# Layer 3's rotary partners by DMA through a scratch array in DRAM instead of by a matmul with a permutation, and its queries and keys three tiles ahead instead of two

## The chip, the cores and the metric

One core of one Trainium2 chip runs the whole program in one launch. The metric is the device time of an execution in microseconds (us). Engines are named as in the profile: PE is the matmul engine (PEld its weight loads), DVE the vector engine, ACT the scalar engine, POOL the GpSimd engine, SP the engine that here only issues DMAs.

## The reference, cut to what matters

Four transformer-like layers run one after another over x of 64 sequences of 64 tokens of 256 features. The change is in the attention of the last of them, layer 3:

```
nx = _ada_rmsnorm(x, time_emb, w_norm1, t1_w1, t1_b1, t1_w2, t1_b2)
q = (nx @ wq + bq).reshape(b, s, N_HEADS, HEAD_DIM)       # 16 heads of 16
k = (nx @ wk + bk).reshape(b, s, N_HEADS, HEAD_DIM)
v = (nx @ wv + bv).reshape(b, s, N_HEADS, HEAD_DIM)
q = q * c + _rotate_half(q) * si                          # rotate_half: [-x2, x1] of the halves of 8
k = k * c + _rotate_half(k) * si
scores = jnp.einsum('bshd,bthd->bhst', q, k) / jnp.sqrt(jnp.float32(HEAD_DIM))
probs = jax.nn.softmax(scores, axis=-1)
attn = jnp.einsum('bhst,bthd->bshd', probs, v).reshape(b, s, D_MODEL)
x = x + attn @ wo + bo
```

Every feature of a query or key needs its partner, the feature 8 places away in the same head of 16.

## The kernel before

All arithmetic is fp32. The 4096 tokens are 32 tiles of 128 tokens (two sequences each), and the layer's attention is straight-line code, written out for the tiles t = 0 to 31. Each engine has its own instruction list, in the order in which its function writes it, and runs it in that order; engines wait for each other by semaphores. `after(engine, L.s["name"], n)` is such a wait: for the signal "name" to have been given n times. So the order of the code below is the order of the work.

In `pe_narrow`, one tile t of PE is: `scores(t)`; `project(t - 2)`, the output projection of two tiles ago; `qk(t + 2)`, queries and keys of two tiles ahead, transposed, features on the partitions, into the one PSUM bank psW1; `turn_probs(t, 0)`, transposes of the first half of the exponentials; `pe_transpose_x(t + 3)`; `values(t + 2)`; `turn_probs(t, 1)`; `rotate(t + 2)`; `outputs(t)`. `rotate` multiplies the biased queries and keys (128 x 512) with a 128 x 128 permutation, `partner`, so that every feature's partner stands on its partition, and it uses psW1 again.

In `act_narrow`, ACT does in tile t: exponentials of half 0; `biased(t + 2)`, four activations that bring psW1 to the buffer qb with the bias; exponentials of half 1; two copies of the turned exponentials to SBUF (signals pta and ptb); `values(t + 2)`, which copies the values out of PSUM; `modulate(t + 3)`, which writes the modulated, normalised input hT. In `dve_narrow`, DVE does the maxima and subtractions of both halves (`dve_softmax`), then `add`, `output`, `measure`, then `sines(t + 2)`, partner times sine, and `dve_norm(t + 4)`. In `pool_narrow`, POOL does cosine times qb, adds the product with the sine (signal qf), and spreads the keys over four head masks (signal mask), all for tile t + 2. Layer 0 runs through the same functions without the rotation.

The buffers hT, qb and qk have two copies each. SP has no DMA to issue between layer 3's loads and the stores of the last feed-forward.

Of the kernel before, what the change touches and what calls it, by code (L numbers as in the profile page):

```python
# [14 lines left out]
P = 128  # L15
# [112 lines left out]
def build_program(nc, A, out):  # L128
    ctx = ExitStack()
    with ctx:  # L130
# [90 lines left out]
        mod_rows = nc.dram_tensor("mod_rows", [B, 2 * D], FP32, kind="Internal").ap()  # L221
        slot_token = nc.dram_tensor("slot_token", [E8 * CAP], I32, kind="Internal").ap()
# [8 lines left out]
        class Attention:  # L231


            def __init__(self, li):
# [30 lines left out]
                if li == 3:  # L265
                    self.sin, self.cos = W.take(4, P), W.take(4, P)
                    self.qk = [W.take(4, P) for _ in range(2)]
                self.g, self.b = table(f"g{li}"), table(f"b{li}")
# [5 lines left out]
                                 3: " qk qke mask vp on xb rot rsin rcos qf"}[li], NT)  # L274
                if li == 1:
                    self.s |= signals("rows_in", NT * 32)
                self.loads = {0: 2, 1: 3, 2: 4, 3: 5}[li]
# [218 lines left out]
        def pe_narrow(pe, L):  # L496
# [5 lines left out]
            def qk(n):  # L502
                after(pe, L.s["h"], n + 1)
                after(pe, L.s["rsin" if rotary else "qke"], n)
                for q in range(4):
                    for k in range(KC):
                        ins = nc.tensor.matmul(psW1[:, q * P:(q + 1) * P], w[:, k, q * P:(q + 1) * P],  # L507
                                               L.hT[n % 2][:, k, :], start=(k == 0), stop=(k == KC - 1))
                ins.then_inc(L.s["qk"].sem, 1)

            def rotate(n):

                after(pe, L.s["qke"], n + 1)
                nc.tensor.matmul(psW1[:, :], partner[:, :], L.qb[n % 2].rearrange("p a b -> p (a b)"), start=True, stop=True
                                 ).then_inc(L.s["rot"].sem, 1)

            def values(n):
# [3 lines left out]
                for b in range(2):  # L521
                    for k in range(KC):
                        for hp in range(2):
                            ins = nc.tensor.matmul(psV[64 * hp:64 * hp + 64, b], L.hT[n % 2][:, k, b * N:(b + 1) * N],
# [217 lines left out]
        def dve_narrow(v, ch, L):  # L742
            rotary = L.li == 3
            def sines(n):

                after(v, L.s["rot"], n + 1)
                after(v, L.s["qf"], n)
                nc.vector.tensor_tensor(by_batch_part(L.sin), psW1[:, :].rearrange("p (a n) -> p a n", n=N), angles(1),
# [1290 lines left out]
```

## Time and profile before

| | before |
|---|---|
| time, median of 3 runs | 2900.86 us (2899.26 to 2901.13) |
| the profiled execution's own time | 2900.1 us |
| its span, first to last instruction | 2898.3 us |
| PE busy | 2621.5 us (90%) |
| DVE busy | 1624.3 us (56%) |
| ACT busy | 1045.3 us (36%) |
| POOL busy | 470.9 us (16%) |
| mean granted PE clock | 0.950 of full speed |

The profile is of one execution. Its span leaves 1.8 us of the execution's time outside. A busy share is a mean over stages with different limits, so for a change in one stage the trace of that stage is read: layer 3's attention, from about 2255 to 2536 us. Lines as L514 are lines of the kernel before. Where an instruction is an fp32 matmul, the trace has more than one record for it, so counts there are of records.

### The profile page before, as it was taken

Reading aid. Unit: us, or ns where it says so; the run is one execution under the profiler, and the core shown is the slowest. Engines: PE = TensorE matmul, PEld = TensorE weight load, DVE = VectorE, ACT = ScalarE, POOL = GpSimd, SP = SyncE. Lnnn points to the kernel's source line nnn. Section 1 sums busy time; section 2 is a strip of 40 time slices with the busy share of each in tenths; the row PEclk is TensorE's granted clock in tenths of the full one; section 3 lists DMA queues with packets and bytes.
Section 4 is the critical chain, followed back from the end, with each engine's and each line's share of the span. In section 5 each row is a group of like instructions: output and inputs, shape, how many; then the busy total and the mean of one; then the engine's idle time right before and its main releaser. Section 6 shows DMA issues by size and latency. Waiting matters only on the chain.

```text
span 2898.3 us, 60070 instructions
## 1 busy us (share of the span) xinstructions
PE 2621.5 (90%) x24108; PEld 1838.6 (63%) x24108; DVE 1624.3 (56%) x3749; ACT 1045.3 (36%) x2095; POOL 470.9 (16%) x402
## 2 busy tenths in 40 slices
PE   6888599999999843999799999997999899889999
PEld 5666366666666532666688888885444677646555
DVE  5888677878777576332355555543332688732221
ACT  4555355655655400212133333332121566510110
POOL 2233010101101001223111111110000566400000
PEclk9999799999999955999899999998999899989999
DMA  5000000000000121333400000000000000000000
GB/s 200 2 2 2 12 23 22 29 29 22 29 22 29 52 84 54 92 92 91 124 0 0 0 0 0 0 0 1 0 0 0 2 2 2 2 8 8 14 15 15
DMA packets 62439, 78.27 MB, mean 27 GB/s; under 512 B 12704, under 2 KB 52128, under 8 KB 61792
## 3 DMA queue, kind: packets, MB, share of 16 engines
q1 hardware_dynamic: 56160, 67.88, 7.1%
q0 software_dynamic: 6144, 8.52, 1.5%
q8 instruction: 92, 1.51, 0.2%
q14 instruction: 43, 0.35, 0.0%
HBM read 59.33 MB, written 17.06 MB: 26 GB/s over the span
## 4 chain that ended last, share of the span: by engine, by line
PE 83%; DVE 10%; ACT 3%; issue 3%; DMA 1%; SPq 0%; POOL 0%; DVEq 0%; POOLq 0%; ACTq 0%
PE psW L301 16%; PE psW L294 8%; PE psS L1268 7%; PE psP L416 4%; PE psP L1234 4%; PE psP L1228 4%; PE psS L1262 4%; PE psO L1228 4%; PE psP L409 4%; PE psO L1234 4%; PE psW L507 3%; PE psS L360 3%; PE psO L393 2%; PE psO L325 2%; PE psP L376 2%
## 5 line engine op out<-in xcount | busy, mean ns | idle before, releaser
L301 PE MATMUL psW<-r,work 128*128 128x512 f32 x1024 | 482.1, 604 | 1.0 <-DVE work L718 1.0
L1162 POOL TENSOR_TENSOR work<-work 128x512 f32<-128x512 f32 x128 | 132.2, 1044 | 1151.8 <-DVE work L740 1151.8
L301 PEld LDWEIGHTS psW<-r,work 128*128 128x128 f32 x1024 | 180.9, 191 | 162.8 <-issue 157.1
L294 PE MATMUL psW<-work,r 128*128 128x128 f32 x2048 | 244.6, 278 | 1.0 <-DVE work L718 1.0
L294 PEld LDWEIGHTS psW<-work,r 128*128 128x128 f32 x2048 | 235.9, 194 | 3.5 <-DVE work L718 1.4
L729 DVE TENSOR_REDUCE work<-psS 128x8 f32<-128x512 f32 x256 | 175.5, 686 | 107.5 <-PE psS L537 74.7
L1268 PE MATMUL psS<-r,work 128*128 128x256 f32 x960 | 211.2, 381 | 5.3 <-DVE work L1338 5.3
L1268 PEld LDWEIGHTS psS<-r,work 128*128 128x128 f32 x960 | 181.2, 190 | 32.8 <-DVE work L1338 6.1
L731 DVE TENSOR_TENSOR work<-psS,work 128x512 f32<-128x512 f32 x256 | 177.1, 692 | 11.3
L1084 ACT ACTIVATE work<-work 128x512 f32<-128x512 f32 x128 | 80.1, 626 | 277.4 <-DVE work L731 277.4
L1140 POOL TENSOR_TENSOR work<-work,head_mask 128x1024 f32<-128x1024 f32 x64 | 121.5, 1899 | 205.2 <-ACT work L1024 202.7
L1418 ACT ACTIVATE work<-psP 128x512 f32<-128x512 f32 x64 | 38.2, 597 | 285.6 <-PE psO L1228 285.6
L1338 DVE TENSOR_TENSOR work<-work,psO 128x512 f32<-128x512 f32 x64 | 44.1, 689 | 168.7 <-ACT work L1418 168.7
L416 PEld LDWEIGHTS psP<-work,r 128*128 128x128 f32 x1024 | 123.8, 195 | 16.2 <-ACT work L1100 8.8
L507 PEld LDWEIGHTS psW<-work,r 128*128 128x128 f32 x1024 | 125.3, 196 | 12.1 <-ACT work L1004 5.9
L507 PE MATMUL psW<-work,r 128*128 128x128 f32 x1024 | 128.9, 280 | 4.3 <-ACT work L1004 3.8
L1040 ACT ACTIVATE work<-work 128x512 f32<-128x512 f32 x128 | 81.1, 634 | 139.7 <-DVE work L731 139.7
L716 DVE TENSOR_TENSOR work<-psW,tab 128x256 f32<-128x256 f32 x64 | 27.0, 421 | 184.6 <-PE psW L287 184.6
L416 PE MATMUL psP<-work,r 128*128 128x128 f32 x1024 | 126.6, 278 | 1.2 <-ACT work L1100 1.2
L409 PE MATMUL psP<-r,work 128*128 128x256 f32 x512 | 126.1, 380 | 1.2 <-ACT work L1100 1.2
L1234 PE MATMUL psP<-work,r 128*128 128x512 f32 x256 | 120.7, 611 | 4.7 <-DVE work L1327 3.0
L1228 PE MATMUL psP<-work,r 128*128 128x512 f32 x256 | 122.2, 600 | 3.0 <-DVE work L1327 3.0
(222 smaller groups left out, 4681.8 us busy)
## 6 DMA issues: line engine op xcount, KB each, us to landing
r<-in_l_fc SPq DMA_DIRECT2D x16, 1024.0 KB, 6.7
work<-mod_rows SPq DMA_DIRECT2D x64, 128.0 KB, 2.8
r<-in_l_w SPq DMA_DIRECT2D x2, 3072.0 KB, 14.8
x<-in_x SPq DMA_DIRECT2D x8, 512.0 KB, 9.6
gather_table<-work SPq DMA_DIRECT2D x32, 128.0 KB, 1.8
moe_sum<-work SPq DMA_DIRECT2D x32, 128.0 KB, 1.7
x<-moe_sum SPq DMA_DIRECT2D x8, 512.0 KB, 7.3
out<-x SPq DMA_DIRECT2D x8, 512.0 KB, 2.9
```

The lines of the kernel that those rows point to most:

```text
L294: ins = nc.tensor.matmul(ps[:, q * P:(q + 1) * P], w[:, k, lo + q * P:lo + (q + 1) * P], L.hT[:, k, :], start=(k == 0), stop=(k == KC - 1))
L301: ins = nc.tensor.matmul(ps[:, 0:width], L.hT[:, k, :], w[:, k, lo:lo + width], start=(k == 0), stop=(k == KC - 1))
L409: ins = nc.tensor.matmul(psP[:, 0:D], L.oT[:, j, :], l1_wout[:, j, :], start=(j == 0), stop=(j == FJ - 1))
L416: ins = nc.tensor.matmul(psP[:, q * P:(q + 1) * P], l2_wout[:, j, q * P:(q + 1) * P], L.oT[:, j, :], start=(j == 0), stop=(j == FJ - 1))
L507: ins = nc.tensor.matmul(psW1[:, q * P:(q + 1) * P], w[:, k, q * P:(q + 1) * P], L.hT[n % 2][:, k, :], start=(k == 0), stop=(k == KC - 1))
L729: ch.link(nc.vector.tensor_reduce(mx, ps, AX.X, ALU.max))
L731: nc.vector.tensor_tensor(L.E[:, 8 * i:8 * i + 8, :], ps, mx.unsqueeze(2).broadcast_to([P, 8, N]), ALU.subtract).then_inc(L.s[f"sub{i}"].s ...
L1140: nc.gpsimd.tensor_tensor(L.kbd[n % 2], k.unsqueeze(2).broadcast_to([P, 4, 4, N]), head_mask[:, 8:12].unsqueeze(1).unsqueeze(3).broadcast_ ...
L1162: nc.gpsimd.tensor_tensor(E, E, halves(L.rs)[i].unsqueeze(2).broadcast_to([P, 8, N]), ALU.mult).then_inc(L.s[f"prob{i}"].sem, 1)
L1228: ins = nc.tensor.matmul(ps, w[:, k, j * P:(j + 1) * P], Q.gT[:, k, :], start=(k == 0), stop=(k == KC - 1))
L1234: ins = nc.tensor.matmul(HB[j % 4], Q.w1[u][:, k, j * P:(j + 1) * P], Q.gT[:, k, :], start=(k == 0), stop=(k == KC - 1))
L1268: ins = nc.tensor.matmul(psS[:, r * D:(r + 1) * D], Q.hid[:, j, r * P:(r + 1) * P], Q.w2[u][:, j, :], start=(j == 0), stop=(j == FJ - 1))
```

## The change

For tiles 2 to 31 the product with the permutation is gone. SP waits for the biased queries and keys of tile n, stores them twice into a scratch array `rotated` in DRAM, so that each head's 16 rows stand there twice in a row, waits for both stores, and loads 16 rows from 8 further down: each feature's partner comes back to its partition, in the new buffer `turned`. DVE's `sines` reads it there, from SBUF instead of from PSUM. Tiles 0 and 1 keep the product. The distance `L.far` by which queries and keys go ahead becomes 3 in layer 3 (it stays 2 in layer 0): hT and qb get three copies, `qk`, `biased` and `modulate` are each called for one tile further ahead, and so are the transposes of x and `dve_norm`. The calls for tile 2 come before the loop. `values` stays two tiles ahead, but in layer 3 it is written after `turn_probs(t, 1)`, where `rotate` was. ACT's order within a tile stays.

```diff
+        rotated = nc.dram_tensor("rotated", [2, 8, 32, 4 * P], FP32, kind="Internal").ap()
...
-                    self.hT = [W.take(KC, P) for _ in range(2)]
-                    self.qb = [W.take(4, P) for _ in range(2)]
+                    self.far = 2 if li == 0 else 3
+                    self.hT = [W.take(KC, P) for _ in range(self.far)]
+                    self.qb = [W.take(4, P) for _ in range(self.far)]
...
+                    self.turned = [W.take(4, P) for _ in range(2)]
...
             def qk(n):
                 after(pe, L.s["h"], n + 1)
-                after(pe, L.s["rsin" if rotary else "qke"], n)
+                after(pe, L.s["qke"], n)
+                if rotary and n <= 2:
+                    after(pe, L.s["rsin"], n)
...
             if rotary:
                 rotate(1)
+                qk(2)
+                pe_transpose_x(pe, L, 3)
...
             for t in range(NT):
                 scores(t)
                 if t > 1:
                     project(t - 2)
-                if t + 2 < NT:
-                    qk(t + 2)
+                if t + L.far < NT:
+                    qk(t + L.far)
                 turn_probs(t, 0)
-                if t + 3 < NT:
-                    pe_transpose_x(pe, L, t + 3)
-                if t + 2 < NT:
+                if t + L.far + 1 < NT:
+                    pe_transpose_x(pe, L, t + L.far + 1)
+                if t + 2 < NT and not rotary:
                     values(t + 2)
                 turn_probs(t, 1)
                 if t + 2 < NT and rotary:
-                    rotate(t + 2)
+                    values(t + 2)
                 outputs(t)
...
             def sines(n):
-                after(v, L.s["rot"], n + 1)
+                if n < 2:
+                    after(v, L.s["rot0"], n + 1)
+                    turned = psW1[:, :].rearrange("p (a n) -> p a n", n=N)
+                else:
+                    after(v, L.s["rot_odd" if n % 2 else "rot_even"], n // 2 * 16)
+                    turned = by_batch_part(L.turned[n % 2])
...
             def biased(n):
                 after(a, L.s["qk"], n + 1)
-                after(a, L.s["qf" if L.li == 3 else "s1"], n - 1)
+                after(a, L.s["qf" if L.li == 3 else "s1"], n + 1 - L.far)
...
             values(1)
+            if L.li == 3:
+                biased(2)
+                modulate(3)
...
                 exps(t, 0)
-                if L.li == 3 and t + 2 < NT:
-                    biased(t + 2)
+                if L.li == 3 and t + 3 < NT:
+                    biased(t + 3)
                 exps(t, 1)
...
+            for n in range(2, NT):
+                u = n % 2
+                after(sp, L[3].s["qke"], n + 1)
+                back = L[3].s["rot_odd" if u else "rot_even"]
+                after(sp, back, (n // 2 - 1) * 16)
+                for copy in range(2):
+                    sp.dma_start(rotated[u, :, 16 * copy:16 * copy + 16, :], rows_of(L[3].qb[n % 3])
+                                 ).then_inc(L[3].s["rot_rows"].sem, 16)
+                after(sp, L[3].s["rot_rows"], (n - 1) * 32)
+                after(sp, L[3].s["rsin"], n - 1)
+                sp.dma_start(rows_of(L[3].turned[u]), rotated[u, :, 8:24, :]).then_inc(back.sem, 16)
```

Where this puts the instructions is seen in the two programs' lists. Line numbers differ between them: `scores`, `project`, `qk`, `turn_probs`, `values`, `outputs` are L537, L572, L507, L547, L524, L557 and L562 before, and L546, L581, L516, L556, L533, L566 and L571 in the change; the product is L514 before, L523 in the change; the transposes of x are L287 and L294. PE, a tile in the middle of layer 3, before, from the first turn of the exponentials to `outputs`:

```order
L547 MATMUL psP<-consts,work 128x128 [waits pta,exp0]
L547 MATMUL psP<-consts,work 128x128 x3
L287 MATMUL psW<-consts,work 128x128 [waits h,xn]
L287 MATMUL psW<-consts,work 128x128
L524 MATMUL psO<-r,work 64x128 [waits xupd,v]
L524 MATMUL psO<-r,work 64x128 x7
L547 MATMUL psP<-consts,work 128x128 [waits ptb,exp1]
L547 MATMUL psP<-consts,work 128x128 x3
L514 MATMUL psW<-work,partner 128x512 [waits qke]
L557 MATMUL psO<-work,pair_sums 32x128 [waits pta,ptb,on,v]
```

The same place of PE's list in the change:

```order
L556 MATMUL psP<-consts,work 128x128 [waits pta,exp0]
L556 MATMUL psP<-consts,work 128x128 x3
L294 MATMUL psW<-consts,work 128x128 [waits h,xn]
L294 MATMUL psW<-consts,work 128x128
L556 MATMUL psP<-consts,work 128x128 [waits ptb,exp1]
L556 MATMUL psP<-consts,work 128x128 x3
L533 MATMUL psO<-r,work 64x128 [waits xupd,v]
L533 MATMUL psO<-r,work 64x128 x7
L566 MATMUL psO<-work,pair_sums 32x128 [waits pta,ptb,on,v]
```

The product is gone, and the eight matmuls of the values stand behind the second turn, the one that waits for exp1, instead of ahead of it.

ACT, the same tile in the change (L1060 exponentials, L1040 `biased`, L1071 the copies, L1032 the values' copies, L1020 `modulate`):

```order
L1060 ACTIVATE work<-work 128x512 [waits sub0]
L1040 ACTIVATE work<-psW,col 128x128 [waits qf,qk]
L1040 ACTIVATE work<-psW,col 128x128 x3
L1060 ACTIVATE work<-work 128x512 [waits sub1]
L1071 ACTIVATE work<-psP 128x512 [waits pv,ta]
L1071 ACTIVATE work<-psP 128x512 [waits pv,tb]
L1032 ACTIVATE heads_v<-psO 64x16x16 [waits pv,vp]
```

Nothing moved in this list within a tile: `biased`, which waits for the signal of `qk`, still stands between the two exponentials; it is now that of tile t + 3.

PE ahead of the first tile, in the change, from `values(1)` to the first tile's `qk`:

```order
L533 MATMUL psO<-r,work 64x128 x7
L523 MATMUL psW<-work,partner 128x512 [waits qke]
L516 MATMUL psW<-work,r 128x128 [waits rsin,qke,h]
L516 MATMUL psW<-work,r 128x128 x7
L294 MATMUL psW<-consts,work 128x128 [waits h,xn]
L294 MATMUL psW<-consts,work 128x128
L546 MATMUL psS<-work 64x256 [waits mask,su_consts,su_bias]
L546 MATMUL psS<-work 64x256 x7
L516 MATMUL psW<-work,r 128x128 [waits qke,h]
```

The first `scores` (L546) stood right behind the product before; now the `qk` of tile 2, with a wait for rsin, and the transposes of tile 3 stand between.

## Rows read from the trace of the kernel before

**Rows 1.** The chain that ended last, by line, 2366 to 2392 us.

```profile
by line: PE psW L507 20.8%; PE psS L537 14.0%; PE psO L572 12.2%; PE psW L514 9.9%; ACT work L1024 9.8%; PE psO L557 8.8%; PE psP L547 7.6%; PE psO L562 6.9%; ACT work L1040 6.1%; issue 4.2%
```

**Rows 2.** Busy time per window; columns: window, length, engines, PE clock, DMA.

```profile
2350.00:2400.00 50.00, 49.55 (x720) 38.13 (x716) 40.03 (x68) 32.89 (x89) 31.22 (x25) 1.00 0.01 2
```

**Rows 3.** Timeline of one tile, PE: start, length, engine, line, what.

```profile
2375.06 1.09 PE L537 MATMUL psS<-work 64*64 64x256 f32 x16
...
2377.05 1.95 PE L507 MATMUL psW<-work,r 128*128 128x128 f32 x16
...
2378.83 0.60 PE L547 MATMUL psP<-consts,work 128*128 128x128 f32 x4
...
2379.27 0.38 PE L287 MATMUL psW<-consts,work 128*128 128x128 f32 x2
...
2379.58 1.09 PE L524 MATMUL psO<-r,work 128*64 128x128 f32 x16
...
2380.75 0.66 PE L547 MATMUL psP<-consts,work 128*128 128x128 f32 x4
...
2381.25 1.02 PE L514 MATMUL psW<-work,partner 128*128 128x512 f32 x2
...
2382.20 0.65 PE L557 MATMUL psO<-work,pair_sums 128*32 128x128 f32 x16
...
2383.22 1.09 PE L537 MATMUL psS<-work 64*64 64x256 f32 x16
```

**Rows 4.** The same tile, ACT.

```profile
2379.03 1.15 ACT L1024 ACTIVATE work<-psW,col 128x128 f32<-128x128 f32 x4 [0.75 <-PE psW L507]
...
2380.05 0.64 ACT L1040 ACTIVATE work<-work 128x512 f32<-128x512 f32 x1
...
2381.45 0.60 ACT L1051 ACTIVATE work<-psP 128x512 f32<-128x512 f32 x1 [0.26 <-PE psP L547]
...
2381.94 0.76 ACT L1016 ACTIVATE heads_v<-psO 64x256 f32<-64x256 f32 x2
...
2382.72 1.30 ACT L1004 ACTIVATE work<-psW,tab 128x64 f32<-128x64 f32 x4
```

**Rows 5.** The same tile, DVE: `sines`, and the next tile's first maximum.

```profile
2382.36 0.69 DVE L748 TENSOR_TENSOR work<-psW,consts 128x512 f32<-128x512 f32 x1 [0.41 <-PE psW L514]
...
2384.37 0.69 DVE L729 TENSOR_REDUCE work<-psS 128x8 f32<-128x512 f32 x1 [1.05 <-PE psS L537]
```

**Rows 6.** Timeline of tile 1, PE: `values`, then the second turn.

```profile
2281.78 1.09 PE L524 MATMUL psO<-r,work 128*64 128x128 f32 x16
...
2282.81 0.66 PE L547 MATMUL psP<-consts,work 128*128 128x128 f32 x4
```

**Rows 7.** Start of the layer: `scores` of tiles 0 and 2, and `sines(1)`.

```profile
2270.12 1.09 PE L537 MATMUL psS<-work 64*64 64x256 f32 x16
...
2270.23 0.69 DVE L748 TENSOR_TENSOR work<-psW,consts 128x512 f32<-128x512 f32 x1 [1.03 <-PE psW L514]
...
2285.28 1.09 PE L537 MATMUL psS<-work 64*64 64x256 f32 x16
```

**Rows 8.** End of the layer: `scores` of tiles 30 and 31.

```profile
2513.81 1.09 PE L537 MATMUL psS<-work 64*64 64x256 f32 x16
...
2521.27 1.09 PE L537 MATMUL psS<-work 64*64 64x256 f32 x16
```

**Rows 9.** DMA issues: count, KB each, median us to landing.

```profile
out<-x SPq DMA_DIRECT2D x8, 512.0 KB, 2.9
...
consts<-in_consts SPq DMA_DIRECT2D x1, 297.5 KB, 2.7
```

**Rows 10.** Timeline of layer 0: PE behind a gap.

```profile
71.12 1.12 PE L547 MATMUL psP<-consts,work 128*128 128x128 f32 x4 [2.69 <-ACT work L1040]
```

**Rows 11.** Two windows of layer 0; the 1.00 or 0.50 is the granted clock.

```profile
71.00:74.40 3.40, 3.28 (x22) 2.72 (x22) 3.33 (x5) 1.18 (x3) 0.00 (x0) 0.50 0.00 0
76.00:100.00 24.00, 21.73 (x330) 17.76 (x329) 18.86 (x34) 15.72 (x43) 7.74 (x6) 1.00 0.01 2
```

More of the change, by code:

```diff
@@ L273, in __init__ @@
                                  2: " prob0 prob1 rsum0 rsum1 i0 i1 i2 i3 e0 e1 e2 e3 v0 v1 v0e ote yt bk",
-                                 3: " qk qke mask vp on xb rot rsin rcos qf"}[li], NT)
+                                 3: " qk qke mask vp on xb rsin rcos qf"}[li], NT)
                 if li == 1:
                     self.s |= signals("rows_in", NT * 32)
+                if li == 3:
+                    self.s |= signals("rot0", 2)
+                    self.s |= signals("rot_rows", (NT - 2) * 32)
+                    self.s |= signals("rot_even rot_odd", (NT - 2) // 2 * 16)
                 self.loads = {0: 2, 1: 3, 2: 4, 3: 5}[li]
@@ L507, in qk @@
                         ins = nc.tensor.matmul(psW1[:, q * P:(q + 1) * P], w[:, k, q * P:(q + 1) * P],
-                                               L.hT[n % 2][:, k, :], start=(k == 0), stop=(k == KC - 1))
+                                               L.hT[n % L.far][:, k, :], start=(k == 0), stop=(k == KC - 1))
                 ins.then_inc(L.s["qk"].sem, 1)
@@ L513, in rotate @@
                 after(pe, L.s["qke"], n + 1)
-                nc.tensor.matmul(psW1[:, :], partner[:, :], L.qb[n % 2].rearrange("p a b -> p (a b)"), start=True, stop=True
-                                 ).then_inc(L.s["rot"].sem, 1)
+                nc.tensor.matmul(psW1[:, :], partner[:, :], L.qb[n].rearrange("p a b -> p (a b)"), start=True, stop=True
+                                 ).then_inc(L.s["rot0"].sem, 1)
             def values(n):
@@ L523, in values @@
                         for hp in range(2):
-                            ins = nc.tensor.matmul(psV[64 * hp:64 * hp + 64, b], L.hT[n % 2][:, k, b * N:(b + 1) * N],
+                            ins = nc.tensor.matmul(psV[64 * hp:64 * hp + 64, b], L.hT[n % L.far][:, k, b * N:(b + 1) * N],
                                                    wv[:, k, :, hp, :], start=(k == 0), stop=(k == KC - 1))
@@ L1000, in modulate @@
                 after(a, L.s["a"], n + 1)
-                after(a, L.s["vp"], n - 1)
+                after(a, L.s["vp"], n + 1 - L.far)
                 for k in range(KC):
                     for b in range(2):
-                        ins = nc.scalar.activation(L.hT[n % 2][:, k, b * N:(b + 1) * N],
+                        ins = nc.scalar.activation(L.hT[n % L.far][:, k, b * N:(b + 1) * N],
                                                    psW0[:, k * P + b * N:k * P + (b + 1) * N], ACT.Identity,
@@ L1021, in biased @@
                 after(a, L.s["qk"], n + 1)
-                after(a, L.s["qf" if L.li == 3 else "s1"], n - 1)
+                after(a, L.s["qf" if L.li == 3 else "s1"], n + 1 - L.far)
                 for q in range(4):
-                    ins = nc.scalar.activation(L.qb[n % 2][:, q, :], psW1[:, q * P:(q + 1) * P], ACT.Identity,
+                    ins = nc.scalar.activation(L.qb[n % L.far][:, q, :], psW1[:, q * P:(q + 1) * P], ACT.Identity,
                                                bias=c(f"l{L.li}_bqk", q))
@@ L1056, in act_narrow @@
                     values(t + 2)
-                if t + 3 < NT:
-                    modulate(t + 3)
+                if t + L.far + 1 < NT:
+                    modulate(t + L.far + 1)
         def act_attention(a, L):
```

11 lines of the change are left out of this document (6 added, 5 removed).

## The prediction

> **What bounds the kernel now.** I looked first at the stage alone, since the change touches only layer 3's attention. In a window of it PE is busy 49.55 of 50 us at the full clock, 1.00, which is 2.4 GHz [rows 2]. Read alone, that says that PE is the limit and that every matmul taken off it is won. The chain of work says something else: the product L514 has 9.9% of it, but 9.8% and 6.1% belong to ACT's L1024 and L1040 [rows 1]. So PE is released by ACT once per tile, and I read one tile in order of time to see where.
>
> From one `scores` to the next is 8.16 us [rows 3]. The steps, each the distance between two starts [rows 3, 4]: `scores` and `project`, 2375.06 to 2377.05, 1.99; `qk` until ACT can begin `biased`, to 2379.03, 1.98; `biased` until the second exponential, to 2380.05, 1.02; that exponential and the hop to PE's second turn, to 2380.75, 0.70; the turn until the product, 0.50; the product until `outputs`, 0.95; `outputs`, 1.02. The sum is 8.16, the whole tile. `values` is not in it. It runs from 2379.58, beside ACT's part, and would let the second turn begin 1.03 later, about 2380.61 [rows 3, 6]; the exponential ends at 2380.69. PE looks full because two limits lie 0.1 us apart: the time PE would need by itself, and the path `qk`, `biased`, exponential, turn.
>
> **The change, part by part.**
>
> *A tile in the middle.* The product and its 0.95 leave PE. But ACT's order stays: `biased`, which waits for this tile's `qk`, stands ahead of the second exponential, so the second turn stays 1.98 + 1.02 + 0.70 behind the start of `qk`. That `biased` now serves a tile further ahead changes nothing in this wait. `values` moves from the place where it hid in that path to one behind the turn, and takes the product's place on it. So instead of 0.50 + 0.95 the path has a turn followed by `values`. The turn: four transposes take 0.44 to the next start when more transposes follow, and two take 0.31 when `values` follows, 0.09 more than their half of 0.44 [rows 3]; so 0.53. `values`: 1.03 to the next start [rows 6]. A tile becomes 8.16 + 0.03 + 0.08 = 8.27. No row shows `values` followed by `outputs`. From below, `outputs` can't start before ACT's last copy ends at 2382.05, which with a hop of 0.06 is 0.09 earlier than now [rows 3, 4]: 8.07. From above I allow another 0.1: 8.37. I take 8.27, since `values` and the transposes keep their rows whoever is next.
>
> *What else hangs on the moved work.* ACT's copies of the values can begin 0.95 later, near 2382.4 instead of 2381.94, and with `modulate` (0.76 + 1.30) end near 2384.4; the next `qk` needs them at 2385.3, the next `project` the copies alone at 2384.3 [rows 3, 4]. Both hold, by 0.9 and more. `sines` no longer waits 0.41 for the product [rows 5]; DVE is ready early anyway (1.05 of waiting before the next maximum), so this is worth nothing. It costs nothing that qb and hT have a third copy. POOL gets its input earlier.
>
> *The DMAs.* They cost nothing while their path is short enough. It starts when `biased` ends (2380.18) and must end when DVE comes to `sines` in the next tile (2381.95 plus a tile of 8.27) [rows 4, 5]: 10.0 us. Two stores of 256 KB each: as many bytes as one store of 512 KB, 2.9 us, and about 0.5 for the second issue. The load: 2.7 us for 297.5 KB [rows 9]. Sum 6.1. From below it can't matter; from above, were all of the 5.6 us of landing streaming and the rate halved, 11.7.
>
> The Trainium skill has a rule against this part (DMA: Bandwidth & Descriptors, "Why a DMA increments its semaphore by 16 and not by 1"): a DMA is spread over the largest number of engines up to 16 that divides the slowest dimension of both sides. The scratch side here is 8 x 16 x 512, so by it 8 engines would carry each of these DMAs. No row here shows such a DMA. By the rule the path lies between 6.1 and 11.7, and the sum stays as it is.
>
> *The start.* Before the first `scores` there is now `qk(2)`, which waits for `sines(1)`, over at 2270.92 [rows 7], and then 1.78 of `qk` and 0.31 of transposes [rows 3]. `scores(0)` moves from 2270.12 to 2273.1. In tile 0, `qk(3)` waits for `modulate(3)`, which on ACT stands behind `biased(2)`: 2271.0 + 1.98 + 1.15 + 1.30 = 2275.4 [rows 4]. From there the path is 1.98 + 1.02 + 0.70 + 0.53 + 1.03 + 1.02 = 6.28: `scores(1)` at 2281.7. In tile 1, `qk(4)` waits for `modulate(4)`, behind the copies of values that moved: values are done at 2280.7, plus 0.76 and 1.30 is 2282.8; 6.28 more gives `scores(2)` at 2289.1. Before, it was 2285.28 [rows 7]. Loss 3.9. Bounds: 2.2 if only the added `qk` and transposes counted, 5 if the waits cost more hops.
>
> *The end.* The last `qk` is now in tile 28. Tile 29 then looks like tile 30 before, which took 7.46 instead of 8.16 [rows 8]. Gain 0.7; nothing, if `values(31)` isn't hidden in it.
>
> *Sum.* Tiles 2 to 28 are 27: 27 x 0.11 = +3.0. With the start, +3.9, and the end, -0.7: +6.2 us. The profiled execution took 2900.1 by its own time: 2906.3. The median of the runs is 0.8 higher: **2907**. A measurement of this kernel tells about 0.2%, 5.8 us, from no change; the forecast lies just beyond that, a slight loss.
>
> **The rivals.**
>
> *Faster: PE was the limit.* If the second turn follows the transposes as soon as PE is free, a tile loses the product: 8.16 - 0.95 = 7.21. Then 27 x -0.95, +3.9 and -0.7 give -22: 2878. For it: [rows 2]. Against: the turn starts 0.06 after the exponential ends, and ACT is in the chain in every tile. It decides if ACT could do `biased` without waiting for the same tile's `qk`. 6 in 100.
>
> *The tile gets no longer.* If `outputs` follows the last copy, 8.07: -2.4 + 3.9 - 0.7, a result of 2902. Part of the forecast's own range, 2901 to 2911.
>
> *The DMAs come late.* The loop that closes: path, `sines` and the norm (2.01 less 1.05 of waiting, 0.96), then from the maximum to the end of `biased` (2384.37 to 2388.34, less 0.75 of waiting, 3.2): 4.2 in all, within two tiles, 16.5 [rows 4, 5]. So a path over 12.3 us makes every tile longer by half of what is over: at 14 us, 0.85 x 29 = +25, with the rest 2931. The upper bound above is 11.7. 7 in 100.
>
> *The clock falls.* With `values` gone from there, PE stands still from 2379.58 to 2380.75 in every tile, 1.17 us, where it waited 0.1 before [rows 3]. In layer 0 it idled 2.69 us and then ran at clock 0.50, 1.2 GHz, for 3.4 us [rows 10, 11]; with 2.3 us of idling in 24 the clock was 1.00. The new gaps are between, and nearer to the second. A fall costs up to 1.7 us: in five tiles +8.5, 2916; in all 27, 2953. 8 in 100. The Trainium skill (TensorE: Matmul & The Clock Gate, "A second HAM failure mode: psum-queue depth-cycling") tells of a kernel in which short idles between groups of matmuls, often enough, made the clock go up and down; layer 0's window at 1.00 shows that such idling doesn't do it always.
>
> **How the numbers follow.** Forecast 0.79, of its range about 0.43 above 2906.7 and 0.36 below; late DMAs 0.07 and clock 0.08 slower; PE the limit 0.06 faster. Slower 0.58, same 0.36, faster 0.06. The range 2900 to 2916 takes in the forecast's bounds and a clock that falls in a few tiles.
>
> **What would show it.** In the trace after: tiles 8.27 apart; a gap of about 1.1 us on PE before the second turn, released by ACT's exponential; `values` between it and `outputs`; `biased` still released by `qk`; `sines` waiting for nothing; `scores(2)` 4 us later; clock 1.00. Wrong would be: a second turn that doesn't wait for ACT, DVE idle before `sines`, or a clock under 1.00.

## The result, and the profile after

The changed kernel takes 2910.79 us (median of 7 runs, 2906.41 to 2913.19); the kernel before, beside it, 2899.26 (7 runs, 2897.55 to 2901.55). The ratio is 1.0038, interval 1.0027 to 1.0048: slower, and by more than the 0.2% that a measurement can tell. The forecast was 2907, 6.2 above before; the loss is 11.5. The profiled execution took 2912.28, 12.2 more than that of before.

The page of the kernel after: busy time of each engine (first row), the group of the two turns of the exponentials (second: busy, mean ns | idle before, and what ended it), and the new DMAs (count, KB each).

```profile
PE 2600.9 (89%) x24048; PEld 1833.6 (63%) x24048; DVE 1622.3 (56%) x3749; ACT 1048.7 (36%) x2095; POOL 469.5 (16%) x402
...
L556 PE MATMUL psP<-consts,work 128*128 128x128 f32 x512 | 84.2, 289 | 58.3 <-ACT work L1060 58.3
...
rotated<-work SPq DMA_DIRECT2D x60, 256.0 KB
...
work<-rotated SPq DMA_DIRECT2D x30, 256.0 KB
```

The second row counts both layers that run through this line: 58.3 us in which PE stands still, with the turn next in its list, until ACT's exponential is over. 37.9 of them lie between 2250 and 2540, in layer 3; the kernel before waits 4.2 us there for the same thing.

PE in a tile in the middle, after (start, length, engine, line, what, in brackets the idle time ahead and what ended it); the answer of before is [rows 3].

```profile
2375.73 1.09 PE L546 MATMUL psS<-work 64*64 64x256 f32 x16
2376.76 1.13 PE L581 MATMUL psO<-r,work 128*128 128x256 f32 x4
2377.72 1.95 PE L516 MATMUL psW<-work,r 128*128 128x128 f32 x16
2379.51 0.60 PE L556 MATMUL psP<-consts,work 128*128 128x128 f32 x4
2379.95 0.38 PE L294 MATMUL psW<-consts,work 128*128 128x128 f32 x2
2381.42 0.66 PE L556 MATMUL psP<-consts,work 128*128 128x128 f32 x4 [1.10 <-ACT work L1060]
2382.01 1.09 PE L533 MATMUL psO<-r,work 128*64 128x128 f32 x16
2383.03 0.64 PE L566 MATMUL psO<-work,pair_sums 128*32 128x128 f32 x16
2383.49 0.63 PE L571 MATMUL psO<-work,heads_v 128*32 128x64 f32 x32
2384.05 1.09 PE L546 MATMUL psS<-work 64*64 64x256 f32 x16
```

ACT in the same tile, after ([rows 4] before):

```profile
2379.71 1.14 ACT L1040 ACTIVATE work<-psW,col 128x128 f32<-128x128 f32 x4 [0.75 <-PE psW L516]
2380.73 0.64 ACT L1060 ACTIVATE work<-work 128x512 f32<-128x512 f32 x1
```

From `scores` to `scores` it is 8.32, by the starts 1.99 + 1.99 + 1.02 + 0.69 + 0.59 + 1.02 + 1.02: the path through `qk`, `biased`, exponential and second turn that the prediction draws, with the 1.10 of standing still just where `values` used to be.

SP's DMAs and DVE's `sines` with the next maximum, after ([rows 5] before):

```profile
2380.88 1.20 SPq L1913 DMA_DIRECT2D rotated<-work  x2
2386.36 0.60 SPq L1917 DMA_DIRECT2D work<-rotated  x1
```

```profile
2385.20 0.69 DVE L740 TENSOR_REDUCE work<-psS 128x8 f32<-128x512 f32 x1 [1.59 <-PE psS L546]
...
2390.98 0.69 DVE L764 TENSOR_TENSOR work<-work,consts 128x512 f32<-128x512 f32 x1
```

The stores are issued at 2380.88, the load only 5.5 later, and `sines`, which needs the load, begins 10.1 after the stores without a wait.

The start of the layer, after: PE, then DVE ([rows 7] before). The first `scores` is 18.2 behind the layer's first transposes; before it was 15.1.

```profile
2274.43 1.09 PE L546 MATMUL psS<-work 64*64 64x256 f32 x16
2276.70 2.05 PE L516 MATMUL psW<-work,r 128*128 128x128 f32 x16 [1.17 <-ACT work L1020]
...
2283.13 1.09 PE L546 MATMUL psS<-work 64*64 64x256 f32 x16
...
2288.33 0.66 PE L556 MATMUL psP<-consts,work 128*128 128x128 f32 x4 [1.91 <-ACT work L1060]
...
2292.51 1.09 PE L546 MATMUL psS<-work 64*64 64x256 f32 x16
```

```profile
2285.33 0.69 DVE L764 TENSOR_TENSOR work<-work,consts 128x512 f32<-128x512 f32 x1 [7.02 <-DMA work<-rotated]
...
2286.20 0.68 DVE L740 TENSOR_REDUCE work<-psS 128x8 f32<-128x512 f32 x1
```

In tile 0 DVE stands for 7.02 us in `sines(2)`, until the first load has landed. Tile 1's maximum is behind it in DVE's list and comes at 2286.20, though its `scores` began at 2283.13, and PE's turns of tile 1 wait in their turn. That is a wait which the prediction does not have.

Where the 12.2 us of the two profiled executions lie, in distances between starts of PE:

| stretch | before | after | difference |
|---|---|---|---|
| ahead of layer 3 (its first transposes) | 2255.02 | 2256.21 | +1.2 |
| to `scores(0)` | 15.10 | 18.22 | +3.1 |
| tile 0 | 7.58 | 8.70 | +1.1 |
| tile 1 | 7.58 | 9.38 | +1.8 |
| 27 tiles in the middle | 8.16 | 8.32 | +4.3 |
| tile 29 | 8.16 | 7.46 | -0.7 |
| tile 30 | 7.46 | 8.31 | +0.9 |
| behind `scores(31)` | 377.0 | 377.5 | +0.5 |

The first row is not the change: nothing ahead of layer 3 differs, and over the profiled executions of the kernels below these first transposes stand between 2249.5 and 2256.6. So the experiments are also compared by the length of the layer, from its first transposes to `scores(31)`: 266.3 before, 276.8 after. Each such length is from one profiled execution. Where the DMAs don't make the tiles uneven it repeats (276.8 and 276.7 in the kernel after and e2, 274.6 in e4 and e7); in the others it is one sample.

### The profile page after: what moved, and what is told of

Same layout as the page of the kernel before. It is cut to its first block, busy times and chain, and to the rows that moved or that the text cites. A ratio compares the mean times of both kernels' runs of the same rounds, so it can differ in the third digit from the quotient of the medians.

```text
span 2910.5 us, 60096 instructions
## 1 busy us (share of the span) xinstructions
PE 2600.9 (89%) x24048; PEld 1833.6 (63%) x24048; DVE 1622.3 (56%) x3749; ACT 1048.7 (36%) x2095; POOL 469.5 (16%) x402
## 4 chain that ended last, share of the span: by engine, by line
PE 83%; DVE 10%; issue 3%; ACT 3%; DMA 1%; SPq 0%; POOL 0%; DVEq 0%; ACTq 0%; POOLq 0%
PE psW L308 16%; PE psW L301 8%; PE psS L1288 7%; PE psP L423 4%; PE psP L1254 4%; PE psP L1248 4%; PE psS L1282 4%; PE psP L416 4%; PE psO L1248 4%; PE psO L1254 4%; PE psW L516 3%; PE psS L367 2%; PE psO L400 2%; PE psO L332 2%; PE psP L383 2%
## 5 line engine op out<-in xcount | busy, mean ns | idle before, releaser
L742 DVE TENSOR_TENSOR work<-psS,work 128x512 f32<-128x512 f32 x256 | 176.9, 691 | 11.3
L556 PE MATMUL psP<-consts,work 128*128 128x128 f32 x512 | 84.2, 289 | 58.3 <-ACT work L1060 58.3
L516 PEld LDWEIGHTS psW<-work,r 128*128 128x128 f32 x1024 | 125.3, 196 | 14.6 <-ACT work L1020 9.4
L516 PE MATMUL psW<-work,r 128*128 128x128 f32 x1024 | 129.0, 280 | 6.0 <-ACT work L1020 4.8
L1060 ACT ACTIVATE work<-work 128x512 f32<-128x512 f32 x128 | 81.1, 633 | 134.7 <-DVE work L742 134.6
L1254 PE MATMUL psP<-work,r 128*128 128x512 f32 x256 | 120.7, 611 | 4.7 <-DVE work L1347 3.0
## 6 DMA issues: line engine op xcount, KB each, us to landing
rotated<-work SPq DMA_DIRECT2D x60, 256.0 KB
work<-rotated SPq DMA_DIRECT2D x30, 256.0 KB
```

The lines of the kernel that those rows point to most:

```text
L742: nc.vector.tensor_tensor(L.E[:, 8 * i:8 * i + 8, :], ps, mx.unsqueeze(2).broadcast_to([P, 8, N]), ALU.subtract).then_inc(L.s[f"sub{i}"].s ...
L1254: ins = nc.tensor.matmul(HB[j % 4], Q.w1[u][:, k, j * P:(j + 1) * P], Q.gT[:, k, :], start=(k == 0), stop=(k == KC - 1))
```

## The experiments

Theory A, that of the prediction: the middle tile is bound by the path `qk`, `biased`, exponential, turn, because ACT's `biased` stands ahead of the second exponential; what left PE was not on it, and `values`, put behind the turn, is. B: PE by itself is the limit. C: the DMAs cost the time, by their waits or by what they load. Four kernels, run together (before 2897.23, 23 runs):

**e1_exp_first**, the kernel after, ACT's order swapped:

```
                 exps(t, 0)
+                exps(t, 1)
                 if L.li == 3 and t + 3 < NT:
                     biased(t + 3)
-                exps(t, 1)
```

> The changed kernel with ACT's second exponential ahead of the four activations that bring queries and keys out of PSUM, nothing else. Path theory (the second exponential waits behind them, and they wait for this tile's queries and keys): the exponential ends about 1.05 us earlier in a tile, the second turn no longer waits for it, and the next limit is ACT's copies, now behind those activations: a tile of about 7.8 us instead of 8.32, some 14 us less than the changed kernel. Rival, the DMA path of 9.8 us sets the tile: it now starts 0.5 us later, so a tile stays at 8.3 or gets longer, and DVE waits for the DMA in every tile. Rival, PE's own work is the limit: 8.3, no change.

Measured: 2900.14 (10 runs), 1.0009 of before (1.0000 to 1.0019); layer 269.7. Most middle tiles are 7.72, but eight are 7.85 to 11.3, and tile 1 is 12.05. The waits in the layer, and DVE's in tile 0:

```profile
DVE work L764 <- DMA work<-rotated: 33.9, 27, 6.9
```

```profile
2279.41 0.69 DVE L764 TENSOR_TENSOR work<-work,consts 128x512 f32<-128x512 f32 x1 [6.91 <-DMA work<-rotated]
```

A is confirmed by the 7.72, 0.60 less per tile from ACT's order alone. But the tile is now short enough for the DMAs to be late: 27 waits, where the kernel after has 6. The longest tiles, 12.05 and 11.3, hold a second cost. While PE stood still for 2.88 us ahead of the first turn of tile 1, the granted clock fell to 0.50 and stayed there for 6.8 us (the window below lies in them). In the tile of 11.3 it was at 0.50 for 3.4 us.

```profile
2282.00:2288.00 6.00, 5.59 (x62) 4.69 (x66) 4.03 (x6) 4.15 (x12) 4.52 (x4) 0.50 0.30 81
```

**e2_dead_product**, the kernel after with a product of the same size, whose result nobody reads, between transposes and second turn:

```
                     pe_transpose_x(pe, L, t + L.far + 1)
+                if rotary and t + 2 < NT:
+                    for i in range(2):
+                        nc.tensor.matmul(psW0[:, 256:512], partner[:, :],
+                                         L.qb[(t + 2) % 3][:, 2 * i:2 * i + 2, :].rearrange("p a b -> p (a b)"),
+                                         start=True, stop=True)
```

> The changed kernel with the permutation product put back on PE, in two halves into an unused part of a PSUM bank, right behind the transposes of x, that is in the gap ahead of the second turn; nobody reads it. Path theory: the gap is 1.10 us and the product takes 0.95, so the tile stays at 8.32, at most 8.4, 0 to 2 us in all. Rival, PE's own work is the limit: 0.95 us more in each of 30 tiles, +28 us.

Measured: 2909.97 (5 runs), 1.0042 (1.0027 to 1.0056); the middle tile is 8.32 again, the layer 276.7. The turn's wait went down to 0.23 instead, in this kernel's timeline of PE:

```profile
2375.82 0.59 PE L616 MATMUL psW<-work,partner 128*128 128x256 f32 x2
2376.65 0.66 PE L556 MATMUL psP<-consts,work 128*128 128x128 f32 x4 [0.23 <-ACT work L1065]
```

B falls for the changed kernel: the product costs nothing where PE waits.

**e3_values_back**, the kernel after with `values` ahead of the second turn:

```
-                if t + 2 < NT and not rotary:
+                if t + 2 < NT:
                     values(t + 2)
                 turn_probs(t, 1)
-                if t + 2 < NT and rotary:
-                    values(t + 2)
                 outputs(t)
```

> The changed kernel with the values' matmuls ahead of the second turn again, where they stood before. Path theory: they hide in the 1.10 us gap, and the path has the turn and ACT's last copy in place of the turn and the values: a tile of 8.07 to 8.1, 6 to 7 us less than the changed kernel, which is the tile of before or slightly under it. Rival, the DMA path sets the tile: no change, 8.32.

Measured: 2906.83 (10 runs), 1.0033 (1.0023 to 1.0042); middle 8.14, layer 272.7, 4.1 less than the changed kernel where 6 to 7 were expected. In its timeline `outputs` now waits for ACT's last copy:

```profile
2377.17 0.64 PE L566 MATMUL psO<-work,pair_sums 128*32 128x128 f32 x16 [0.78 <-ACT work L1069]
```

So with the product gone and `values` back in its place the tile goes from 8.16 to 8.14: the product had hidden behind ACT's copies too. The copy starts 2376.43 and takes 0.60; `outputs` starts 0.14 behind its end, where I had counted with 0.06.

**e4_no_dma**, the kernel after without the scratch array; `sines` reads qb itself, so tiles 2 to 31 get wrong partners (the rotation is left out):

```
-            for n in range(2, NT):
...
-                    after(v, L.s["rot_odd" if n % 2 else "rot_even"], n // 2 * 16)
-                    turned = by_batch_part(L.turned[n % 2])
+                    after(v, L.s["qke"], n + 1)
+                    turned = by_batch_part(L.qb[n % 3])
```

> The changed kernel without its 90 DMAs: the sine product of tiles 2 to 31 reads the queries and keys themselves instead of their partners, so the rotation is left out of the result for these tiles. Path theory: the tile in the middle stays at 8.32; only the wait of 7.02 us in tile 0, which makes tile 1 take 9.38, goes: about 1.7 us less in all. Rival, the DMAs lengthen every tile (by a wait, or by slowing the engines): the tile falls to 8.16 or under, 5 us less or more.

Measured: 2906.61 (7 runs), 1.0032 (1.0020 to 1.0043); middle 8.32, tile 1 7.66 instead of 9.38, layer 274.6. In the middle the DMAs cost nothing; at the start they cost 1.7. In the changed kernel C holds for tile 1 alone. The other 0.4 of the layer's 2.2 is in tile 30, 7.95 for 8.31, in which the clock fell to 0.50 in both.

The next four, together (before 2897.33, 22 runs):

**e5_before_exp_first**, the kernel before with the same swap on ACT (`exps(t, 1)` ahead of `biased(t + 2)`).

> The kernel before with ACT's second exponential ahead of the four activations that bring queries and keys out of PSUM; the product stays on PE. If PE's own work was the other limit, 0.1 us under the path through ACT, a tile becomes 8.06 instead of 8.16, about 3 us less in all. If the path through ACT was the only limit that mattered, much more: 7.5 or so per tile, 15 us less.

Measured: 2898.38 (10 runs), 1.0000 (0.9991 to 1.0010); middle 8.02, layer 263.4, 2.9 less than before. The gain of the layer, 0.1%, is below what the whole time can show. Here B is true: with ACT out of the way PE has no gap left.

```profile
2300.00:2500.00 200.00, 200.00 (x2800) 155.38 (x2800) 163.55 (x274) 132.37 (x350) 127.61 (x101) 1.00 0.01 2
```

So 8.02 is what PE needs by itself with the product, and a tile below it is to be had only by taking work off PE.

**e6_exp_first_no_dma**, e1 without DMAs as in e4 (the rotation of tiles 2 to 31 left out).

> The changed kernel with the second exponential first and without the 90 DMAs (the sine product of tiles 2 to 31 reads the queries and keys themselves, so the rotation is left out there). What remains with neither the product nor the DMA path. If the DMA path is what makes the tiles of the run with the exponential first irregular (up to 12.05 us), they are now even, 7.7 us or, where ACT's copies don't limit, down to 7.5; layer 3 gets some 10 us shorter than there. If ACT and PE make them so, nothing changes.

Measured: 2890.56 (10 runs), 0.9976 (0.9967 to 0.9986); all middle tiles but one 7.72 or 7.73 (the one 7.91), tile 1 7.72, layer 258.2. What made e1 uneven were its DMAs: 11.5 us of layer. The falls of the clock are in this number: without the DMAs the clock stays at 1.00 from 2264 to 2512.

**e7_product_tile2**, the kernel after with tile 2's partners from the product (into the second half of psP, so that tile 0's second turn waits for `sines(2)`), the DMAs from tile 3 on:

```
+                if rotary and t == 0:
+                    rotate(2)
...
-            for n in range(2, NT):
+            for n in range(3, NT):
```

> The changed kernel with tile 2 done by the product as well, in another PSUM bank, in PE's gap in tile 0, so that the DMAs begin with tile 3. Theory: DVE's wait of 7.02 us in tile 0 goes and tile 1 takes 7.7 us instead of 9.38, all else stays: 1.7 us less than the changed kernel. Rival: the start of the layer is slow for another reason, tile 1 stays over 9.

Measured: 2907.92 (7 runs), 1.0033 (1.0020 to 1.0045); tiles 0 and 1 are 8.70 and 7.66, middle 8.32, layer 274.6. The rotation is whole here, and tile 1 is as short as without DMAs: its 1.7 was the wait in tile 0.

**e8_longer_path**, the kernel after with a third store of 256 KB per tile, ahead of the load (with a larger scratch array and the signal's count to match):

```
-                for copy in range(2):
-                    sp.dma_start(rotated[u, :, 16 * copy:16 * copy + 16, :], ...
+                for v, copy in ((u, 0), (2 + u, 0), (u, 1)):
+                    sp.dma_start(rotated[v, :, 16 * copy:16 * copy + 16, :], ...
```

> The changed kernel with a third store of 256 KB per tile, into a spare array that nobody reads, between the two, which the load waits for too. The path from the queries to DVE gets about 2 us longer, near 11.9. By the loop worked out in the prediction a tile gets longer only over about 12.3: DVE waits up to 1.8 us in each tile, and a tile stays at 8.32 or up to 8.4. If the path has no room beyond the 0.3 us that the changed kernel's trace shows ahead of the sine product, a tile becomes longer by 1 to 2 us, 27 to 50 in all.

Measured: 2925.05 (one run, the profiled one); layer 293.8. Fourteen of the 27 middle tiles stay 8.32, but tile 1 is 13.2 and the other thirteen are 8.4 to 11.1. DVE's waits between 2300 and 2500:

```profile
DVE work L764 <- DMA work<-rotated: 44.9, 22, 3.5
```

Half a hit. From the stores' issue to `sines` the path is now 11.2 to 13.7. In the middle waits of up to 2.2 us, with a path of 12.3, left the tile at 8.32, which is where the prediction's loop puts the limit. But the loop gives half of what is over, 0.3 for the three paths of 12.9 to 13.0 in a row (2331.9 to 2350.4), and the tiles behind them took 1.1, 1.0 and 2.4 more. In the last of these the clock had fallen to 0.50 (2368.5 to 2371.9), as in tile 1. So the loop has the limit about right and the cost above it too low.

Then the versions that the runs pointed to. **e9_best** is e1 and e7 together (before 2900.20, 15 runs).

> The changed kernel with two edits: ACT does the second exponential ahead of `biased`, and tile 2's partners come from the product again (into psP, which is free there), so that the scratch array starts with tile 3. From the runs so far: a tile in the middle 7.72 from one `scores` to the next as in e6_exp_first_no_dma, tile 1 7.7 instead of 9.38, no wait of DVE for a DMA in tile 0, and from the first `scores` of the layer to the last some 240 us as in e6 against about 251 before. That would be 8 to 11 us under the kernel before, 0.996 to 0.997 of it. The rival: the DMAs' path of 9.8 us has, with tiles of 7.72, less room than in the changed kernel, so DVE still waits for the load in many tiles and the clock falls after the longer gaps, as in e1_exp_first; then the time stays at that of the kernel before or of e1, 0.998 to 1.001. The difference between the two is in the number of waits of DVE for the load: none or few, or again some 27.

Measured: 2895.96 (11 runs), 0.9984 (0.9975 to 0.9993); tile 1 is 7.72, but seven middle tiles are 0.13 to 3.0 over, the layer 264.9. The rival came true, in part: 28 waits for the load. Behind the longest of them, in the row below, comes the tile of 10.76, with the clock at 0.50 from 2490.9 to 2494.3.

```profile
2485.82 0.69 DVE L768 TENSOR_TENSOR work<-work,consts 128x512 f32<-128x512 f32 x1 [3.07 <-DMA work<-rotated]
```

The last three ran together (before 2900.03, 22 runs). **e10_norm_first** is e9 with DVE's `dve_norm(t + L.far + 2)` ahead of `sines(t + 2)`.

> e9_best with DVE's norm of tile t + 5 (0.35 us) ahead of `sines`, so that the load has 0.35 us more before DVE waits for it and before the next tile's maximum is late. In e9_best the middle tiles were 7.72 but for seven that were 0.13 to 3.0 over, 7.1 us in all. If the DMAs' path is what lengthens these, those over by little vanish and the others lose up to 0.35 each: about 2 us less in the layer, 262 to 264 from its first transposes to the last `scores`. If something else does, nothing changes (265).

Measured: 2896.95 (11 runs), 0.9993 (0.9984 to 1.0003). The middle tiles' excess fell from 7.1 to 3.8 us and the waits from 30.8 to 21.8, but tile 0 rose to 8.83 and the clock fell in the end tiles (tile 29 9.60): layer 265.0, nothing won. Why tile 0 rose is in the trace: the norm, now ahead, waits 1.24 us for PE's transposes, `sines(2)` ends 6.1 behind `scores(0)` instead of 4.5, and PE's second turn waits 1.14 for it.

**e11_four_ahead** is e9 with queries and keys four tiles ahead:

```
-                    self.far = 2 if li == 0 else 3
+                    self.far = 2 if li == 0 else 4
...
                 pe_transpose_x(pe, L, 3)
+                qk(3)
+                pe_transpose_x(pe, L, 4)
...
                 biased(2)
                 modulate(3)
+                biased(3)
+                modulate(4)
```

> e9_best with queries and keys four tiles ahead instead of three (four copies of hT and qb, one more `qk` and turn ahead of the first `scores`), so that the DMAs have a whole tile more. If their path of 9.8 us is what makes e9_best's tiles uneven, DVE waits for no load and all middle tiles are 7.72, as in e6_exp_first_no_dma where there were no DMAs. The start costs another 2.9 (the first `scores` at 21.0 behind the layer's first transposes instead of 18.1), one tile more at the end is 7.46. The layer then: 258.2 + 2.9 - 0.3 = 261 from the first transposes to the last `scores`, against 264.9 in e9_best and 266.3 before; the time 3 to 4 us under e9_best's. If the uneven tiles are not from the DMAs, they stay, and the layer is 267.

Measured: 2897.41 (11 runs), 0.9993 (0.9984 to 1.0002). All 26 full tiles are 7.71 or 7.72, and DVE never waits for a DMA: the DMAs' path was the cause of the uneven ones. But the layer is 264.8, since the start took 24.2 and not 21.0. Its timeline of PE, and a window in it (its 0.50 is the granted clock):

```profile
2275.50 3.38 PE L516 MATMUL psW<-work,r 128*128 128x128 f32 x16 [2.19 <-ACT work L1027]
...
2279.24 1.14 PE L546 MATMUL psS<-work 64*64 64x256 f32 x16
```

```profile
2276.10:2279.30 3.20, 3.20 (x20) 2.87 (x18) 0.00 (x0) 0.38 (x2) 0.14 (x1) 0.50 0.00 0
```

The added `qk` waits 2.19 for `modulate(4)`, and runs at 1.2 GHz: 3.38 instead of 2.02. A tile at the end lost another 1.4 to the clock.

**e12_copies_first** is e11 with `biased` behind ACT's two copies, where layer 0 has it:

```
                 exps(t, 1)
-                if L.li == 3 and t + 4 < NT:
-                    biased(t + 4)
                 for i, (turned, copied) in enumerate((("ta", "pta"), ("tb", "ptb"))):
...
-                if L.li == 0 and t + 2 < NT:
-                    biased(t + 2)
+                if t + L.far < NT:
+                    biased(t + L.far)
```

> e11_four_ahead with ACT's `biased` behind its two copies of the turned probabilities instead of ahead of them. In e9_best PE still waits 0.41 us per tile for the second copy before `outputs`, and `biased` (1.0) stands ahead of it on ACT. With `biased` behind, that wait should go: 7.31 per tile in place of 7.72, 27 x 0.41 = 11 us less than e11_four_ahead, about 250 in the layer. The room of the DMAs shrinks by the 1.1 us that `biased` moves back, which four tiles ahead leave to spare. Against it: if PE by itself or the path of the second exponential takes 7.7, nothing is won. The second turn starts 4.6 behind `scores` by both, so they are level there; I expect 7.3 to 7.4.

Measured: 2890.63 (6 runs), 0.9970 (0.9958 to 0.9982); every middle tile 7.46 or 7.47, layer 256.0, 10.2 under before. PE in a middle tile, from its `scores` to the next:

```profile
2399.89 1.09 PE L546 MATMUL psS<-work 64*64 64x256 f32 x16
...
2403.66 0.60 PE L558 MATMUL psP<-consts,work 128*128 128x128 f32 x4
...
2404.49 0.66 PE L558 MATMUL psP<-consts,work 128*128 128x128 f32 x4
...
2405.08 1.09 PE L533 MATMUL psO<-r,work 128*64 128x128 f32 x16
...
2406.33 0.64 PE L568 MATMUL psO<-work,pair_sums 128*32 128x128 f32 x16 [0.16 <-issue]
...
2407.35 1.09 PE L546 MATMUL psS<-work 64*64 64x256 f32 x16
```

The turn follows the transposes at once and the idle time ahead of `outputs` is 0.16, with no releaser that the profile shows. PE is close to being the limit again:

```profile
2300.00:2500.00 200.00, 192.53 (x2929) 156.34 (x2928) 175.02 (x292) 138.80 (x365) 135.05 (x107) 1.00 0.34 106
```

Now the product's absence is worth something: 7.46 is 0.56 under the 8.02 that PE alone needed with the product in e5. This order of ACT with the product kept was not run; e5's full PE says only that its tile could hardly be under 8.02. The 7.31 that I expected had no wait left at all. This is the best version, and the only one with the whole rotation that is more than 0.2% under the kernel before.

## Why the prediction was right, and where it was off

**The bound.** Right: with PE 49.55 of 50 us busy [rows 2] the limit was a path that PE's busy time hid. In the change PE is busy 173.7 of 200 us and the kernel is slower; a product back in the gap costs nothing (e2), and the place of `biased` on ACT 0.60 per tile (e1). The second limit that the prediction saw 0.1 under the path, PE's own work, is there as well (e5).

```profile
2300.00:2500.00 200.00, 173.68 (x2656) 142.91 (x2652) 158.29 (x266) 130.52 (x337) 122.19 (x96) 1.00 0.34 97
```

**A tile in the middle.** The mechanism is right, the term a little small: 8.27 was forecast, 8.32 measured. `values` took 1.02 for 1.03, but the turn 0.59 for 0.53, as the four transposes behind a wait are busy 0.66 and not 0.60. Over 27 tiles +4.3 instead of +3.0. The lower bound of 8.07, from the last copy, can't be had either: e3 shows 8.14. One side remark is wrong and harmless: the copies of the values were to begin 0.95 later, but by the prediction's own times it is 0.5 (2382.4 for 2381.94), and the trace has 0.5.

**The start.** "Loss 3.9" (by its own times, 2289.1 less 2285.28, 3.8): 6.0 measured. Two of its steps are right, `scores(0)` +3.1 for +3.0 and tile 0 8.70 for 8.6. The step that failed is the one of tile 1, "`scores(2)` at 2289.1", which makes tile 1 7.4. It has all waits of PE on ACT and none of DVE on the DMA. The sum of the DMAs' room was made for a middle tile alone; in tile 0 DVE comes to `sines(2)` at 2278.3, 2.8 behind the stores' issue at 2275.55. Two terms had to be wrong for this to cost anything, the room in tile 0 and the length of the path: with the 6.1 that the prediction took, DVE would still have waited 3.3 of the 7.02, but tile 1's maximum would not have been late. e4 and e7 show that the wait costs 1.7. "DVE idle before `sines`" was one of the prediction's own signs of being wrong; for tile 0 it was.

**The DMAs.** "They cost nothing while their path is short enough" held by 0.3 us. The sum of 6.1 is the term that was mis-sized most: in tile 0 the stores are issued at 2275.55 and DVE is released at 2285.33, 9.8. It is within the bound of 11.7. The stores took 5.5 until the load could be issued (3.4 in the sum), the load 4.3 (2.7). The sum had taken the landing times of other transfers over as they stood, neither of them through such a scratch array. The room was right, 10.1 for 10.0. Six waits, 9.5 us in all, 7.02 of them in tile 0, are what is seen of it in the changed kernel; e1 and e8 show how near it stood. That it cost nothing in the middle was therefore partly luck: the margin in the sum was 3.9.

**The end.** Tile 29 -0.7, as forecast. Tile 30 is +0.9 and not in the sum: the clock fell to 0.50 at 2529.8, in it, and in the kernel before only at 2528.6, behind `scores(31)`. The rival "the clock falls" had this in the middle tiles, where it did not happen: 1.00 in the row above, with 1.10 of standing still in each. In the kernels whose DMAs were late it did happen in the middle (e1, e8, e9). In tile 30 PE stands still three times:

```profile
2527.95 0.66 PE L556 MATMUL psP<-consts,work 128*128 128x128 f32 x4 [1.12 <-ACT work L1060]
2529.27 0.66 PE L556 MATMUL psP<-consts,work 128*128 128x128 f32 x4 [0.67 <-ACT work L1060]
2531.11 1.08 PE L566 MATMUL psO<-work,pair_sums 128*32 128x128 f32 x16 [1.18 <-DVE work L771]
```

These three can't be the whole reason, for the kernel before has them in its tile 30 as well, at a clock of 1.00:

```profile
2517.09 0.66 PE L547 MATMUL psP<-consts,work 128*128 128x128 f32 x4 [1.12 <-ACT work L1040]
2518.41 0.66 PE L547 MATMUL psP<-consts,work 128*128 128x128 f32 x4 [0.67 <-ACT work L1040]
2520.25 0.64 PE L557 MATMUL psO<-work,pair_sums 128*32 128x128 f32 x16 [1.18 <-DVE work L756]
```

One thing that differs is the tile ahead: without a `qk`, tile 29 of the change already has waits of 1.12 and 0.67, where that of before has one of 0.24. What the clock fell for is not shown. The 0.9 are its price: from `outputs` to `scores(31)` it is 1.87 at 0.50 and 1.02 before. The Trainium skill's account of short idles that send the clock up and down (TensorE: Matmul & The Clock Gate, "A second HAM failure mode: psum-queue depth-cycling") is not borne out by the 27 middle tiles; tile 30 neither shows nor excludes it.

**The sum.** Forecast +3.9 + 3.0 - 0.7 = +6.2; in the traces 6.0 + 4.3 - 0.7 + 0.9 = 10.5 in the layer. The other 1.7 of the 12.2 lie outside it. That 2910.79 falls into the forecast's own 2901 to 2911 is luck in part: the loss of 11.5 is nearly twice the 6.2, and the kernel before took 1.6 less in the result's runs than the 2900.86 from which the forecast counts. Where the gain went that one expects of a product less on PE: 0.95 per tile went into the 1.10 of standing still at the turn, and `values`, which had filled that time, was put on the path.

## What to carry to other kernels

When an engine is busy 99% of a stage, follow one period of it by start times before taking work off it: a path through another engine can be just as long, and then the work taken off turns into a wait. Here the order of two instructions on ACT decided what removing the product was worth: -0.14 per tile for the order alone (e5), -0.02 for the product alone (e3), -0.70 for product and both changes of ACT's order with four tiles of lead (e12). Work out a transfer's room for the first tile as well as for the steady one, and give it more than its mean length, as lengths scatter and a late one can cost a fall of the clock on top of its wait (e1, e8, e9, against e11); but the added tile of lead was paid for at the start, 6.2 us in e11 (24.2 against e9's 18.1). And where the time ahead of the changed stage wanders by 7 us from run to run, compare the stage itself.

## What the runs showed of the hardware

The new DMAs move data at about half the rate of the weight loads. Windows of the kernel after (the last three columns: granted clock, DMA share, GB/s): the load's packets, a pause, the stores' packets, the pause after them, in which the next load is issued, and the first packets of a later load. Then, in a fence of its own, a window of the same kernel's layer 0, in which weights are loaded.

```profile
2380.50:2381.00 0.50, 0.00 (x0) 0.00 (x0) 0.50 (x1) 0.50 (x3) 0.00 (x0) 1.00 0.52 205
...
2381.50:2382.00 0.50, 0.50 (x4) 0.34 (x4) 0.47 (x3) 0.36 (x1) 0.00 (x0) 1.00 0.00 0
...
2384.00:2385.00 1.00, 1.00 (x26) 0.51 (x16) 0.00 (x0) 1.00 (x4) 0.92 (x2) 1.00 0.52 193
...
2386.00:2387.00 1.00, 1.00 (x10) 0.97 (x10) 1.00 (x2) 0.35 (x1) 1.00 (x2) 1.00 0.00 0
...
2396.00:2396.50 0.50, 0.50 (x7) 0.50 (x7) 0.50 (x2) 0.15 (x1) 0.50 (x1) 1.00 0.70 66
```

```profile
20.00:40.00 20.00, 16.58 (x145) 13.66 (x149) 5.26 (x11) 11.88 (x33) 4.47 (x3) 1.00 1.04 395
```

At their full rate these DMAs show shares of about 0.5 and some 200 GB/s, against 1.04 and 395 GB/s for the weights. That is what 8 of the 16 engines would give, an estimate from the two rates. By the Trainium skill (DMA: Bandwidth & Descriptors, "Why a DMA increments its semaphore by 16 and not by 1") a scratch side of 8 x 16 x 512 gives these DMAs 8 engines: the trace agrees in the rate. The share alone doesn't count engines: in the first packets of a load it is 0.70, at only 66 GB/s.

The rate is not even half of the 9.8 us: 768 KB at 200 GB/s would take 3.9, an estimate. In the trip whose stores are issued at 2380.88 the first packets come 1.2 us later and flow until about 2385.7, at 37 to 102 GB/s in the first 1.5 us; the load is issued at 2386.36, some 0.6 behind the last of them, its first packets come 1.2 us after that, and its first microsecond is slow again (37 to 53 GB/s). Whether a scratch array laid out for 16 engines would let three tiles of lead do was not tried.

Two copies of 256 KB to DRAM and one back took 9.8 us from the first issue to the release of the reader in tile 0, where no load was under way when the stores were issued. What scatters are the stores. In e9 the load takes 4.0 to 4.5 from its issue to the release of DVE in all 28 waits, while the stores take 5.3 to 7.9 from their issue until the load is issued; the wait of 3.07 is behind stores of 7.87. Part of it may be how closely stores follow the load before them. In the kernel after they take 6.2 when issued 0.65 or 1.47 behind a load (tiles 3 and 4) and 5.5 in most tiles, where they are issued 2.8 behind it. It is not all: the stores of 7.87 in e9 were issued 2.0 behind a load, and others there at 2.2 took 5.5. What makes those long is open.
